# The routed experts' stage of a two-layer model: its turn in another order, zero products in TensorE's waits, groups marked by matching, first requests moved up

## The reference

```python
scores = jax.nn.sigmoid(x @ router_w.T)                     # 800 tokens x 64 experts
sfc = scores + e_bias[None, :]
group_scores = jax.lax.top_k(sfc.reshape(T, 8, 8), 2)[0].sum(-1)
_, gidx = jax.lax.top_k(group_scores, 4)                    # 4 of 8 groups are kept
masked = jnp.where(smask > 0, sfc, 0.0)                     # smask: gidx as ones, repeated 8 times
_, topk_idx = jax.lax.top_k(masked, 8)
w = jnp.take_along_axis(scores, topk_idx, axis=1)
w = w / (w.sum(-1, keepdims=True) + 1e-20) * 2.5            # scattered to coef, T x 64
h = jax.nn.silu(jnp.einsum('th,ehi->tei', x, Wg)) * jnp.einsum('th,ehi->tei', x, Wu) * coef[:, :, None]
moe_out = jnp.einsum('tei,eih->th', h, Wd)
shared = jax.nn.silu(x @ SWg) * (x @ SWu) @ SWd
```

## Time and profile before

| | us |
|---|---|
| median of 3 runs | 727.19 |
| lowest and highest | 724.03, 727.21 |
| the profiled execution, its own time | 726.52 |
| its span, first to last instruction | 724.7 |
| its mean granted TensorE clock | 0.936 |
| busy: TensorE, VectorE, ACT, GpSimd | 618.8, 388.7, 398.6, 249.0 |

### The profile page before, as it was taken

The page is one execution under the profiler, slowest core; times in us unless marked ns, Lnnn a source line. Parts: engine busy times, 40 slices in busy tenths (PEclk is TensorE's granted clock), DMA queues, the critical chain, the costliest instruction groups (busy, mean ns, idle before and its releaser), DMA issues.

```text
span 724.7 us, 14858 instructions
## 1 busy us (share of the span) xinstructions
PE 618.8 (85%) x4634; PEld 488.5 (67%) x4635; DVE 388.7 (54%) x1148; ACT 398.6 (55%) x952; POOL 249.0 (34%) x326
## 2 busy tenths in 40 slices
PE   3999799999750999989999999999498599999994
PEld 1877466666450888986788756666366588888884
DVE  5222567777643111117988745454864566666662
ACT  1444699989741333335576696876251355555552
POOL 5011455555308000002100000000044588888883
PEclk9999699999955899999999999999679799999999
DMA  6118100000076288403110010000024666666665
GB/s 148 46 31 259 37 2 2 2 2 2 1 241 240 91 290 287 152 30 93 33 47 6 1 50 1 1 1 2 0 91 107 178 172 171 178 170 180 174 172 132
DMA packets 71339, 69.28 MB, mean 96 GB/s; under 512 B 10892, under 2 KB 64873, under 8 KB 71162
## 3 DMA queue, kind: packets, MB, share of 16 engines
q1 hardware_dynamic: 64256, 59.99, 27.2%
q0 software_dynamic: 4272, 6.55, 4.5%
q10 hardware_dynamic: 2762, 2.11, 1.0%
HBM read 56.99 MB, written 11.64 MB: 95 GB/s over the span
## 4 chain that ended last, share of the span: by engine, by line
PE 52%; ACT 11%; POOL 10%; issue 10%; DVE 10%; DMA 3%; SPq 1%; DVEq 1%; POOLq 0%; ACTq 0%
ACT probs L769 4%; PE psum L1112 4%; PE psum L1125 4%; PE psum L617 3%; PE psum L631 3%; PE psum L1599 3%; PE psum L1621 3%; PE psum L1608 3%; PE psum L708 3%; DMA v_all<-in_L_ffn_W_dram 3%; PE psum L1647 2%; PE psum L698 2%; POOL sum_dram L2370 2%; POOL we_low L2355 2%; POOL h_low L2363 2%
## 5 line engine op out<-in xcount | busy, mean ns | idle before, releaser
L769 ACT ACTIVATE probs<-probs,negmax 100x361 f32<-100x361 f32 x128 | 68.9, 587 | 10.8 <-POOL probs L814 10.7
L822 DVE TENSOR_SCALAR_CACHE_REDUCE probs<-psum 100x361 f32<-100x361 f32 x128 | 60.7, 531 | 19.1 <-PE psum L698 19.1
L708 PEld LDWEIGHTS psum<-ident,probs 100*128 100x128 f32 (+1 forms) x384 | 39.7, 157 | 27.6 <-issue 19.8
L708 PE MATMUL psum<-ident,probs 100*128 100x100 f32 (+1 forms) x384 | 48.1, 264 | 11.4 <-ACT probsT L777 4.8
L1153 ACT ACTIVATE kT_all<-psum,kT_all 128x128 f32<-128x128 f32 x88 | 25.1, 368 | 52.0 <-PE psum L1112 52.0
L2185 PE MATMUL psum<-xT_high,we_high 128*128 128x400 f32 x128 | 45.4, 355 | 9.0 <-DVE v_all L2437 8.2
L814 POOL TENSOR_SCALAR probs<-probs 100x722 f32<-100x722 f32 x64 | 50.6, 790 | 5.1
L1112 PE MATMUL psum<-kT_all,v_all 128*128 128x128 f32 x352 | 44.0, 286 | 7.5 <-DMA v_all<-in_L_ffn_W_dram 2.9
L1112 PEld LDWEIGHTS psum<-kT_all,v_all 128*128 128x128 f32 x352 | 42.6, 201 | 10.4 <-issue 6.6
L2070 POOL TENSOR_TENSOR xT_low<-kT_all,xT_high 128x1600 fp32r<-128x1600 f32 x1 | 3.6, 3571 | 130.9 <-ACT xT_high L2047 130.9
L2186 PE MATMUL psum<-xT_low,we_high 128*128 128x400 f32 x128 | 45.0, 351 | 0.0
(11 more groups left out here) (419 smaller groups left out, 1630.5 us busy)
## 6 DMA issues: line engine op xcount, KB each, us to landing
v_all<-in_L_ffn_W_dram SPq DMA_DIRECT2D x16, 1024.0 KB, 7.9
kT_all<-coefT_dram SPq DMA_DIRECT2D x18, 400.0 KB, 4.5
v_all<-in_L_ffn_Wg_dram SPq DMA_DIRECT2D x34, 128.0 KB
v_all<-in_L_ffn_Wu_dram SPq DMA_DIRECT2D x34, 128.0 KB
v_all<-in_L_ffn_Wd_dram SPq DMA_DIRECT2D x34, 128.0 KB
ctx_nat<-in_ctx_dram SPq DMA_DIRECT2D x16, 192.0 KB
xs_dram<-zeros SPq DMA_DIRECT2D x1, 2048.0 KB, 7.7
rank_rows<-rank_dram SPq DMA_DIRECT2D x18, 100.0 KB
```

The costliest lines, as they stand in the source:

```text
L708: last = nc.tensor.transpose(pT_ps[0:rows[t], t, hh * NQ:(hh + 1) * NQ], probs[:, n % NPB, hh, t * P:t * P + rows[t]], ident[0:NQ, 0:NQ])
L769: last = nc.scalar.activation(row, row, ACT.Exp, bias=negmax[:, n % NPB, hh:hh + 1])
L822: last = nc.vector.tensor_scalar(probs[:, n % NPB, hh, 0:NKV], psum[0:NQ, n % 2 * 2 + hh, 0:NKV], -CLAMP, None, ALU.max, ALU.max, accum_ou ...
```

## The change

The turn (`act_experts1`, `pool_experts1`, `dve_experts1`, `sp_experts1`): ACT's first silu comes ahead of the small weights' first split, and the small experts are split in the order 0, 1. GpSimd does the low parts of both halves of the first dense expert ahead of `add_second`, and of the second dense expert only half 0; half 1 is done by VectorE in a new function `last_low`, ahead of `small_hidden`. VectorE splits small weights k behind half k of the first dense expert. SP requests the small weights of turn i + 1 in turn i, around the rank rows, and no longer waits for `row_of_ready`. The down weights get a semaphore of their own, `wd_loaded`.

The first turn: SP requests gate and up of both experts with only the first's down weights, then ranks, coef, and then the second's down weights and the small weights. GpSimd adds its zeros ahead of the first splits.

Zeros: `pe_attend1` multiplies 128x128 zeros by 128x256 zeros once, twice and once ahead of the three finishing steps of the last batch, and 16 times behind them.

Groups: the four best groups are found by MAX8 over the 8 group sums and marked by MATCH_REPLACE8.

Ranks and counts: the shared expert's first down products go behind the counts and the ranks, coef is computed right behind the expert list, its divisor ahead of the counts; the ranks are rounded and stored by ACT (Relu), not VectorE and GpSimd. `route_step` counts to 5 instead of 7, coef being step 4 and `n_used` step 5. Some semaphores are merged.

```diff
@@ pe_attend1
+        def products_of_zeros(count):
+            for _ in range(count):
+                nc.tensor.matmul(score_ps[0][:, 0, 0:D], zeros[:, 0:P], zeros[:, :], start=True, stop=True)
...
-        for s in range(3):
+        pe.wait_ge(A1.max_ready, N1)
+        for s, waiting in enumerate((1, 2, 1)):
+            products_of_zeros(waiting)
             finish[s](B - 1)
+        products_of_zeros(16)
@@ sp_experts1
         sp.wait_ge(route_step, 3)
-        dense = [load(0, p) for p in range(2)]
-        sp.wait_ge(route_step, 4)
+        sp.wait_ge(we_split, 4)
+        dense = [sp.value_load(expert_list[0:1, 0:1], min_val=0, max_val=E1 - 1)]
+        load_gate_up(0, dense[0])
+        dense.append(sp.value_load(expert_list[0:1, 1:2], min_val=0, max_val=E1 - 1))
+        load_down(0, dense[0])
+        load_gate_up(1, dense[1])
+        sp.wait_ge(route_step, 5)
         total = sp.value_load(n_used[0:1, 0:1], min_val=0, max_val=E1)
         sp.wait_ge(ranks_stored, 16)
         for k in range(2):
-            load_rank(0, k, small_at(sp, total, 0, k), True)
+            load_rank(k, small_at(sp, total, 0, k))
         sp.wait_ge(coefT_stored, 16)
         for p in range(2):
             load_coef(0, p, dense[p])
+        load_down(1, dense[1])
+        for k in range(2):
+            load_small(0, k, small_at(sp, total, 0, k))
...
-                        for k in range(2):
-                            load_small(i, k, small_at(sp, total, i, k))
                         dense = [load(i + 1, p) for p in range(2)]
                         load_coef(i + 1, 0, dense[0])
+                        load_small(i + 1, 0, small_at(sp, total, i + 1, 0))
                         for k in range(2):
-                            load_rank(i + 1, k, small_at(sp, total, i + 1, k))
+                            load_rank(k, small_at(sp, total, i + 1, k))
+                        load_small(i + 1, 1, small_at(sp, total, i + 1, 1))
                         load_coef(i + 1, 1, dense[1])
@@ pe_shared
-        for half in range(2):
-            down(0, half)
-        pe.wait_ge(sh_g_taken, 4)
-        pe.wait_ge(sh_u_taken, 4)
+        pe.wait_ge(sh_taken, 5)
         pe.wait_ge(route_step, 1)
...
+        pe.wait_ge(sh_taken, 8)
         rank_picks(0, 0, 5)
         pe.wait_ge(route_step, 2)
         nc.tensor.matmul(r_list_ps, e_col, place[:, :], start=True, stop=True).then_inc(route_sums, 1)
-        pe.wait_ge(route_step, 3)
         rank_picks(1, 5, B)
+        down(0, 0)
...
-        pe.wait_ge(route_step, 5)
+        pe.wait_ge(route_step, 4)
...
         last.then_inc(route_sums, 1)
+        down(0, 1)
         for half in range(2):
             down(1, half)
@@ act_shared
+        act.wait_ge(consts_ready, N_SPARSE + 1)
+        for half, cols in enumerate((slice(0, 5 * NQ), slice(5 * NQ, B * NQ))):
+            act.wait_ge(route_sums, (2, 4)[half])
+            nc.scalar.activation(ranks[0:E1, cols], ranks1_ps[half], ACT.Relu, bias=unranked).then_inc(route_taken, 1)
+        act.wait_ge(route_taken, 2)
+        act.dma_start(rank_dram, ranks).then_inc(ranks_stored, 16)
         act.wait_ge(sh_h_ready, 4)
-        act.wait_ge(route_step, 5)
+        act.wait_ge(route_step, 4)
@@ dve_route1
-        nc.vector.tensor_tensor(ij(work1), other, mine, ALU.is_gt)
-        step(dve, nc.vector.tensor_tensor(ij(work2), other, mine, ALU.is_equal))
...
-        step(dve, nc.vector.tensor_scalar(group_kept[:, :, :], group_kept[:, :, :], float(TOPG), None, ALU.is_lt))
+        for b in range(B):
+            last = nc.vector.max(top8[:, b, :], group_sum[:, b, :])
+        step(dve, last)
+        step(dve, nc.vector.tensor_copy(best_groups[:, :, 0:TOPG], top8[:, :, 0:TOPG]))
+        for b in range(B):
+            last = nc.vector.match_replace(out=group_kept[:, b, :], in_to_replace=best_groups[:, b, :],
+                                           in_values=group_sum[:, b, :], imm_value=-FLT_MAX)
+        step(dve, last)
+        step(dve, nc.vector.tensor_scalar(group_kept[:, :, :], group_kept[:, :, :], -FLT_MAX, None, ALU.is_equal))
@@ act_experts1, split_down and the turn
+            act.wait_ge(wd_loaded[p], 16 * i + 16)
...
-                        split_small(i, 1)
                         silu(i, 0, 0)
+                        split_small(i, 0)
                         high(i, 0, 0)
                         silu(i, 0, 1)
-                        split_small(i, 0)
+                        split_small(i, 1)
                         high(i, 0, 1)
@@ pool_experts1, the turn
                         gather(i)
-                        hidden(i, 0, 0)
+                        for half in range(2):
+                            hidden(i, 0, half)
                         add_second(i)
-                        hidden(i, 0, 1)
-                        for half in range(2):
-                            hidden(i, 1, half)
+                        hidden(i, 1, 0)
@@ dve_experts1
+        def last_low(i):
+            n = 2 * i + 1
+            dve.wait_ge(h1_high_ready, 2 * n + 2)
+            dve.wait_ge(y1_in_psum, 4 * n + 4)
+            dve.wait_ge(h1_ready, 2 * n + 3)
+            nc.vector.tensor_tensor(h1_low[1][:, HT:2 * HT], h1T[:, HT:2 * HT], h1_high[1][:, HT:2 * HT].bitcast(F32),
+                                    ALU.subtract).then_inc(h1_ready, 1)
...
-                        hidden(i, 0)
-                        for k in (1, 0):
+                        for k in range(2):
+                            hidden(i, 0, k)
                             split_small(i, k)
-                        hidden(i, 1)
+                        for half in range(2):
+                            hidden(i, 1, half)
                         for k in range(2):
                             rows_low(i, k)
+                        last_low(i)
                         for k in range(2):
                             small_hidden(i, k, small[k])
```

More of the change, by code:

```diff
@@ L386, in build @@
     we_loaded = [sem(f"we_loaded{p}") for p in range(2)]
+    wd_loaded = [sem(f"wd_loaded{p}") for p in range(2)]
     tables_stored, ranks_stored = sem("tables_stored"), sem("ranks_stored")
@@ L1905, in load_coef, with load_rank @@
                          ).then_inc(coef_loaded[p], 16)
-        def load_rank(i, k, n, first=False):
-            if not first:
-                sp.wait_ge(row_of_ready, 3 * i + k - 2)
+        def load_rank(k, n):
             e = sp.value_load(rank_list[0:1, bass.ds(n, 1)], min_val=0, max_val=E1)
@@ L2084, in dve_route1 @@
     def dve_route1(dve):
+        best_groups = work2[:, :, 0:G1]
+        mark(nc.vector.memset(best_groups[:, :, TOPG:], FLT_MAX))
         mark(nc.vector.memset(expert_list[:, E1:], 0))
@@ L2133, in dve_route1 @@
         step(dve, nc.vector.tensor_reduce(weight_sum[:, :], work1, AX.X, ALU.add))
+        step(dve, nc.vector.tensor_scalar(weight_sum[:, :], weight_sum[:, :], 1e-20, None, ALU.add))
+        step(dve, nc.vector.reciprocal(weight_sum[:, :], weight_sum[:, :]))
         dve.wait_ge(route_sums, 1)
@@ L2150, in dve_route1 @@
         nc.vector.tensor_copy(expert_list[:, 0:E1], r_list_ps).then_inc(route_step, 1)
+        nc.vector.scalar_tensor_tensor(coef, work1, SCALE2, weight_sum[:, :].unsqueeze(2).broadcast_to([NQ, B, E1]),
+                                       ALU.mult, ALU.mult).then_inc(route_step, 1)
         step(dve, nc.vector.tensor_scalar(pairs_below, fours, least, None, ALU.is_lt))
@@ L2153, in dve_route1 @@
         nc.vector.tensor_scalar(n_used[:, :], pairs_n, 2.0, None, ALU.mult).then_inc(route_step, 1)
-        step(dve, nc.vector.tensor_scalar(weight_sum[:, :], weight_sum[:, :], 1e-20, None, ALU.add))
-        step(dve, nc.vector.reciprocal(weight_sum[:, :], weight_sum[:, :]))
-        nc.vector.scalar_tensor_tensor(coef, work1, SCALE2, weight_sum[:, :].unsqueeze(2).broadcast_to([NQ, B, E1]),
-                                       ALU.mult, ALU.mult).then_inc(route_step, 1)
-        for half, cols in enumerate((slice(0, 5 * NQ), slice(5 * NQ, B * NQ))):
-            dve.wait_ge(route_sums, (2, 4)[half])
-            nc.vector.tensor_scalar(ranks[0:E1, cols], ranks1_ps[half], RANKED - 1, 0.0, ALU.subtract, ALU.max
-                                    ).then_inc(route_step, 1)
     def pe_experts1(pe):
-        pe.wait_ge(route_step, 4)
         pe.wait_ge(x_split, X_LOW)
-        pe.wait_ge(coefT_taken, 2)
-        pe.wait_ge(route_step, 7)
+        pe.wait_ge(route_taken, 4)
         def gate_up(i, p):
@@ L2362, in hidden @@
             pool.wait_ge(y1_in_psum, 4 * n + 4)
+            if p == 0 and half == 0:
+                pool.wait_ge(h1_ready, 4 * i + 2)
             nc.gpsimd.tensor_tensor(h1_low[p][:, tok], h1T[:, tok], h1_high[p][:, tok].bitcast(F32), ALU.subtract
@@ L2398, in pool_experts1 @@
         pool.sem_inc(h1_ready, 2)
-        pool.wait_ge(route_step, 7)
-        pool.dma_start(rank_dram, ranks).then_inc(ranks_stored, 16)
+        pool.wait_ge(to_row_ready, 1)
+        add_rows(0, zeros[:, :])
```

(4 more changed lines are left out.)

109 lines of the change are left out of this document (53 added, 56 removed).

## The result

The changed kernel takes 715.91 us (median of 4, 712.74 to 717.23) against 727.2 (724.03 to 727.99): ratio 0.9848, 95% interval 0.981 to 0.9885. So it is faster by 11.3 us, not by the 22.5 forecast, and lies outside the range of 697 to 714. In a second series, beside e4, e6 and e7, it took 714.25 us (ratio 0.984, 0.9814 to 0.9867).

A forecast was written before the change was run, and what follows sets the result against it. Bounds: the expert loop's turns, turn 0's stop and the router at 1.2 GHz. Turn 1 12.0 us sooner plus 10.5 over seven turns is 22.5 us, giving 704.0 and 704.7 from 726.5 and 727.2; forecast 704.5, range 697 to 714.

The forecast's parts named there:

- The zeros: Router: zero products hold TensorE's clock at 2.4 GHz, 0.47 us each; the sigmoid comes 3.3 us sooner.
- Picks are ready at 544.16 - 3.3 - 2.2 = 538.7: Router's end: picks move from 544.16 to 538.7, by 3.3 us from the zeros and 2.2 from the groups.
- The term of the groups: Router, VectorE: marking groups by MAX8 and matching instead of six operations of 4.57 us gains 1.4 to 2.2, taken 2.2.
- These go behind the ranks: 1.3 us: Counts: shared experts' down products, moved behind the ranks, no longer delay the counts; gain 1.3 us.
- stay hidden if the clock holds: Ahead of the counts: shared gate matmuls, 10.7 us from 525.9, end at 536.6 with 2 us of slack.
- Turn 0: First turn: ACT waits for the second expert's Wd until 555.9, silu 556.3, TensorE resumes 558.2; turn 1 starts 12.0 us sooner.
- The ranks on ACT: Ahead of turn 0: two Relu of 0.5 us each on ACT, needing no table load; cost put at nothing.
- The turn: Expert loop: 16.8 us a turn instead of 18.3, last_low taken at 1.1 us; 10.5 us over seven turns.
- The end: From the last turn to the kernel's end: no step in the prediction, change of 0.
- (a): Rival, chance 0.12: the zeros don't hold the router's clock; turn 1 starts 12.3 us later than forecast, 717 us.
- (d): Rival, chance 0.03: slower than before, as the landing of the adds closes a loop; 21 us a turn, 733.

The follow-up runs named there:

- e4: Changed kernel with the second dense expert's first down weights requested early, ahead of the ranks and coef: 712.27 us, ratio 0.9802.
- e6: Changed kernel with the groups marked by comparing again, the six operations of the kernel before: 714.84 us, ratio 0.9833.
- e7: Changed kernel with h_low of the second expert's second half on GpSimd again instead of VectorE's last_low: 713.66 us, ratio 0.9814.
- e1: Changed kernel without its 20 products of zeros: 714.7 us, ratio 0.9853.
- e9: Changed kernel with GpSimd's xT_low late, second down weights early, no small weights behind the last turn, x loaded in two halves: 707.46 us, ratio 0.9729.
- e10: The kernel of e9 (four edits together) without the zeros: 707.61 us, ratio 0.975.
- e2: Changed kernel with GpSimd's xT_low moved behind its add of zeros in the first turn: 712.67 us, ratio 0.9818.
- e8: Changed kernel with the shared expert's first down products ahead of the counts again: 716.09 us, ratio 0.9864.
- e5: Changed kernel without the small experts' weights requested for the turn behind the last: 710.75 us, ratio 0.9786.
- e11: Changed kernel with GpSimd's add of the second small expert between the first dense expert's two h_low pieces again: 718.74 us, ratio 0.9892.
- e3: Changed kernel with nine more products of zeros in TensorE's wait ahead of the counts: 714.83 us, ratio 0.9833.

## Why the prediction was wrong, point by point

**The zeros.** Right in their place: the clock held from 509 to the shared products in the changed kernel's profile, a product took 7.07 / 16 = 0.44 us (forecast 0.47), the projection 1.97, and the sigmoid came 3.3 us sooner by the distance from the additions to x, as forecast. What they are worth is another matter: nothing that the times show, with xT_low early (e1) or late (e9 against e10, with the reservation made there).

**The step that failed first** is "Picks are ready at 544.16 - 3.3 - 2.2 = 538.7". They were ready at 542.2. The term of the groups was near: 535.05 to 538.24 is 3.2 us against 4.57, a gain of 1.4, the low end of what I gave, with 0.8 of the miss in the copy (1.04 where I had put 0.2, and where e9 has 0.18; its groups take 2.34 us, the gain of 2.2 that I took). But the stretch from the first add to the groups, which I took as unchanged, grew from 3.6 us (531.98 to 535.61) to 6.7 (528.34 to 535.05). I had measured the contention on two rows, used it for last_low alone, and moved the whole of VectorE's chain under GpSimd's longest operation without asking what it would meet. Before, xT_low ended at 531.8, just ahead of the add; the late sigmoid had kept them apart. By distances the picks moved by 1.6 us where I had 5.5, and the 3.9 us between are what the four slowed operations cost (e2). The term that I had put at nothing is this contention. It is not the whole miss ahead of the turns: by distances turn 1 came 6.7 us sooner where I had 12.0, and with xT_low late (e2) it gains only 2.0 more; the rest lies in turn 0.

**The counts.** "These go behind the ranks: 1.3 us" assumed TensorE busy up to the picks. With the picks late it stood idle for 4.56 us, the products would have been free there (e8), and the clock fell in that wait. I named the slack ("stay hidden if the clock holds") and didn't ask what an idle TensorE costs.

**Turn 0.** That ACT would stand in a wait for the second expert's down weights was right, and so was the order of what followed. The size was off: silu 5.7 us later than forecast. 4.0 of them came from the start of SP's requests (547.65 instead of 543.6), the rest from SP: the fifth of its requests took 1.10 us, and Wd landed 4.6 us after its request at 557.03, with coef ahead. Moving it early only brings up coef (e4). The ranks on ACT cost no table load, as put: the two Relu took 0.67 and 0.51 us, and no such load stands by them.

**The turn.** 16.67 us against 16.8 forecast: right in size. But its grounds were half wrong. last_low took 0.57 us, not 1.1, as GpSimd had just ended its own piece; and it is worth nothing that shows (e7), where I had counted GpSimd's shorter sum in its favour. So the right size is in part luck. The place of the add is worth 0.64 us a turn, which the row's 0.57 had shown (e11). The other 1.0 us, by what the runs leave, belongs to ACT's silu ahead of the split and to the weights requested a turn ahead; that was not tried alone.

**The end.** A step that wasn't there: I put 0 for it. SP's list had grown by six requests ahead of the load of x, 0.77 MB for a turn that doesn't come, and I counted these bytes only as traffic inside a turn. The chain of waits runs through that list up to the load at 695.52, where an add issued at 686.81 with e5's 6.17 us would have landed by 693.0. The shorter turn also brings the end of TensorE's work nearer to the landing of an add that had moved back in the turn. In all 4.5 us, of which e5 gives back 2.5 by the profile and about 4 by the ratios.

**The rivals.** None happened as it was told. (a) had the zeros fail to hold the clock; they held it here, as in eight profiles of the eleven with zeros, and the time is still that of about (a), by another way. (d), the landing of the adds, doesn't set the turn, but it holds e5's end, and e7's turn of 18.04 us began behind a wait for one. (In its working the parts given as about 10.3 us add up to 10.1, and the threshold stands once as 20.1 and once as 20.0; nothing hangs on either.)

**The medians.** 2.5 us of the miss lie between profile and median: the changed kernel's executions spread from 712.7 to 717.2. Two things differ between profiles of kernels with the same order of requests. In the changed kernel's two and in those of e3, e5, e7, e8 and e11, turn 1 starts 65.9 to 67.9 us behind the additions to x; in the changed kernel's (65.9, 66.0) the clock was at 1.2 GHz for some 3 us once TensorE went on, in the others (67.6 to 67.9) for 5.7 us or more. And single turns are longer where a DMA lands late: 17.61 us in the changed kernel's second profile, 17.78 in e9's, where TensorE waited 0.97 and 1.14 us for gathered rows. The profile behind the ledger has no such turn. How the four executions divide between the two causes isn't shown.

## What to carry to other kernels

An engine that is sped up moves the next one's work under something else: before taking the gain, lay the moved stretch beside what GpSimd does at the new time, and price every VectorE operation on SBUF operands there by the time that GpSimd's instruction has left. Work taken out of an engine's list ahead of a wait is only a gain if that engine wasn't about to wait; look at the idle time it leaves, and at the clock in it. When loads are requested a turn ahead, look at what is queued behind them once the loop has ended.

## What the runs showed of the hardware

VectorE beside GpSimd: a 100x512 operation on two SBUF tensors took 0.69 us alone, 1.41 beside a product of 1.05 us, and 2.20 from 528.34 on, as GpSimd's 3.56 us instruction ran to 529.98; it ended 0.56 us behind that one. A copy of 100x32, with one input in SBUF, took 0.18 us in e9, 1.04 from 535.73 on, beside a GpSimd product from 535.70 to 536.73, and 0.64 in e1, from 533.86 on, beside one from 533.43 to 534.46: both end 0.04 us behind the product. Operations of 256 and 64 columns ended 0.29 and 0.08 us behind theirs. So the price is not a factor but what is left of GpSimd's instruction, with the operation's own work behind it. It goes the other way too: GpSimd's product of 1.03 us took 1.43 from 538.38 on, behind a VectorE operation of 512 columns from 538.24 to 538.93. The Trainium skill (Trainium Architecture — The Big Picture, What this means for kernel authors) calls the pair's sharing an exclusive lock, not a split of bandwidth; these rows agree. I had used 1.41 against 0.69 for two inputs only, and never asked how much of GpSimd's instruction was left.

TensorE's clock behind the zeros: in the changed kernel's two profiles and in six others (e3, e4, e5, e7, e8, e11) it held through the transposes and the logits; in e2, e6 and e9 the same instructions, with the same zeros in front, met 1.2 GHz from 523.4 to 524.3 on, for 7 to 10 us. So with 16 products the router ran at 2.4 GHz in eight profiles of eleven; what decides it isn't shown.
